# Masked graph attention: every second chunk of visits 6 to 21 transposed by VectorE, and wider weight buffers in visits 1 to 7

## The reference

```
h   = relu(layernorm(x))                                # row by row
e   = leaky_relu(h @ a[:256] + (h @ a[256:]).T, 0.01)   # 8192 x 8192
att = softmax(where(adj > 0, e, -9e15), axis=1)
out = x + att @ h
```

## Time and profile before

| | |
|---|---|
| median of 3 runs | 1552.14 us (1547.85 to 1553.05) |
| the profiled execution | 1552.08 us, of it span 1550.3 us |
| granted TensorE clock | 0.999 |
| PE busy | 1522.7 us, 98% |
| DVE busy | 1489.6 us, 96% |
| ACT busy | 1162.5 us, 75% |
| POOL busy | 457.4 us, 30% |
| DMA | 331.05 MB, mean 214 GB/s |

### The profile page before, as it was taken

The page is one execution under the profiler, slowest core; times in us unless marked ns, Lnnn a source line. Parts: engine busy times, 40 slices in busy tenths (PEclk is TensorE's granted clock), DMA queues, the critical chain, the costliest instruction groups (busy, mean ns, idle before and its releaser), DMA issues.

```text
span 1550.3 us, 38852 instructions
## 1 busy us (share of the span) xinstructions
PE 1522.7 (98%) x12678; PEld 1511.9 (98%) x12678; DVE 1489.6 (96%) x2172; ACT 1162.5 (75%) x1180; POOL 457.4 (30%) x547
## 2 busy tenths in 40 slices
PE   5999999999999999999999999999999999999999
PEld 5999999999999999999999999999999999999998
DVE  7999999999999999999999999999999999999998
ACT  7787877778777777677776876777777777677774
POOL 6363334335452340120420320320320320420420
PEclk9999999999999999999999999999999999999999
DMA  6666677787778799999999999999999999999994
GB/s 211 222 200 230 206 223 227 230 248 221 245 220 254 220 225 233 221 201 206 218 207 207 224 204 207 226 197 210 230 195 205 228 195 207 217 195 209 219 199 98
DMA packets 436493, 331.05 MB, mean 214 GB/s; under 512 B 16704, under 2 KB 378176, under 8 KB 436416
## 3 DMA queue, kind: packets, MB, share of 16 engines
q1 hardware_dynamic: 411360, 288.94, 83.6%
q10 hardware_dynamic: 25056, 41.13, 8.7%
HBM read 308.90 MB, written 21.10 MB: 213 GB/s over the span
## 4 chain that ended last, share of the span: by engine, by line
PE 82%; DMA 5%; DVE 3%; ACT 3%; issue 2%; SPq 1%; ACTq 0%; DVEq 0%
PE acc L950 27%; PE acc L953 26%; PE acc L952 26%; DMA adj_in<-in_adj_dram 5%; PE T L917 2%; ACT mask L542 2%; DVE w_lo L797 1%; DVE halves L786 1%; SPq L268 1%; ACT w_hi L552 0%; DVE T L767 0%; DVE w_lo L801 0%; ACT w_hi L555 0%; DVE adj_in L901 0%; DVE adj_in L896 0%
## 5 line engine op out<-in xcount | busy, mean ns | idle before, releaser
L950 PE MATMUL acc<-h_hi,w_hi 128*128 128x258 f32 (+1 forms) x4096 | 1167.3, 285 | 9.2 <-DVE w_lo L801 3.4
L953 PE MATMUL acc<-h_hi,w_lo 128*128 128x258 f32 (+1 forms) x4096 | 1153.3, 282 | 0.0
L952 PE MATMUL acc<-h_lo,w_hi 128*128 128x256 f32 (+1 forms) x4096 | 1149.7, 281 | 0.0
L950 PEld LDWEIGHTS acc<-h_hi,w_hi 128*128 128x128 f32 x4096 | 771.8, 188 | 17.8 <-issue 8.0
L952 PEld LDWEIGHTS acc<-h_lo,w_hi 128*128 128x128 f32 x4096 | 778.4, 190 | 0.1
L953 PEld LDWEIGHTS acc<-h_hi,w_lo 128*128 128x128 f32 x4096 | 775.3, 189 | 0.0
L786 DVE SCALAR_TENSOR_TENSOR halves<-r_rep,g_all,T 128x512 f32<-128x512 f32 (+1 forms) x1024 | 712.7, 736 | 10.8 <-PE T L917 1.5
L542 ACT ACTIVATE mask<-adj_in,mhalf 128x2048 fp8e5<-128x2048 int32 x256 | 510.3, 1993 | 58.8 <-DMA adj_in<-in_adj_dram 58.5
L552 ACT ACTIVATE w_hi<-halves 128x1024 fp32r<-128x1024 f32 x336 | 353.6, 1057 | 185.0 <-DVE halves L786 172.3
L797 DVE SCALAR_TENSOR_TENSOR w_lo<-halves,w_hi 128x1024 fp32r<-128x1024 f32 x336 | 418.2, 1245 | 9.9 <-PE acc L953 4.9
L555 ACT ACTIVATE w_hi<-halves 128x1024 fp32r<-128x1024 f32 x176 | 185.3, 1057 | 97.5 <-DVE halves L786 92.6
(11 more groups left out here) (70 smaller groups left out, 343.8 us busy)
## 6 DMA issues: line engine op xcount, KB each, us to landing
adj_in<-in_adj_dram SPq DMA_DIRECT2D x672, 256.0 KB, 5.0
adj_in<-in_adj_dram SPq DMA_DIRECT2D x88, 1024.0 KB, 6.3
part_sums<-stage ACTq DMA_DIRECT2D x24, 516.0 KB, 5.6
xo<-part_sums ACTq DMA_DIRECT2D x24, 516.0 KB, 4.4
r_rep<-r_rows SPq DMA_DIRECT2D x39, 256.0 KB, 4.8
xb<-in_x_dram ACTq DMA_DIRECT2D x15, 512.0 KB, 5.9
out_dram<-xb ACTq DMA_DIRECT2D x15, 512.0 KB, 4.7
xb<-in_x_dram SPq DMA_DIRECT2D x14, 512.0 KB, 5.8
```

The source lines that it names most:

```text
L950: nc.tensor.matmul(acc[:, t, 0:WC], w_hi[:, k % HL, cols], rhs_hi, start=start and u == 0, stop=False)
L952: nc.tensor.matmul(acc[:, t, 0:D], w_hi[:, k % HL, cols], rhs_lo, start=False, stop=False)
L953: last = nc.tensor.matmul(acc[:, t, 0:WC], w_lo[:, k % LL, cols], rhs_hi, start=False, stop=stop and u == 1)
```

## The change

In visits 6 to 21 (iterations 12 to 43) the odd chunk of each iteration is loaded in the order for VectorE and transposed by VectorE, in slot k = 1 between the subtraction (with side work) and the weights. TensorE keeps the even chunks. The forms have names now: PLAIN (TensorE both), ALT (TensorE even, VectorE odd), LATE (VectorE both); the counts that the semaphores are compared with are worked out from the form. In visits 1 to 7 (`wide`) the pairs' weights go to four pairs of halves instead of two buffers; the two halves more lie where `xo` is, so `halves` and `xo` are now one tensor `work`, and the scratch output of the row sums goes to a spare half of the PSUM bank `hs_ps` and into a weight buffer. The half with the older reader is written first (u = 1, then u = 0).

```diff
+    PLAIN, ALT, LATE = (0, 0), (0, 4), (4, 4)
+    N_ALT = 2 * 6
     N_MID = 2 * 22
+    def count_turned_by_tensor(n, kc, form):
+        return n * CI + kc + 1 if form == PLAIN else n + N_ALT + 1
+    def count_turned_by_vector(n, kc, form):
+        return n - N_ALT + 1 if form == ALT else N_MID - N_ALT + (n - N_MID) * CI + kc + 1
...
+        work = sb("work", [P, 8 * BLK + G * WC], f32)
+        halves = work[:, 0:10 * BLK].rearrange("p (n j) -> p n j", j=BLK)
+        xo = work[:, 8 * BLK:].rearrange("p (t w) -> p t w", w=WC)
+        wide_w = [halves[:, 2:4, :], halves[:, 4:6, :], halves[:, 2:9:6, :], halves[:, 4:10:5, :]]
...
             def quarter(v, q, prev, make=None, phase=None, made=None, nxt=None, head=False, turn=False,
-                        dt=MID, dt_next=MID, deep=False):
+                        dt=ALT, dt_next=ALT, deep=False, wide=False, pwide=False):
...
-                for q in range(4 if dt else 0):
-                    sp.dma_start(adj_in[32 * q:32 * q + 32, kc, G - dt:G, :],
-                                 adj_turned[b, :, 4 * (G - dt):4 * G, ds(c * BLK + q * P, P)]).then_inc(s_turn[kc], 16)
+                    sp.dma_start(adj_in[32 * q:32 * q + 32, kc, :, :],
+                                 adj_turned[b, :, :, ds(c * BLK + q * P, P)]).then_inc(s_turn[kc], 16)
...
-                    load_adj(V.b, c + kc, n, kc, not (V.head and first), V.dt)
+                    load_adj(V.b, c + kc, n, kc, not (V.head and first), V.dt[kc])
...
             def transpose_mask(V, n, kc):
-                g = n * CI + kc
-                t = G - V.dt
-                if V.dt < G:
-                    dve.wait_ge(s_T, g + 1)
-                else:
-                    dve.wait_ge(s_mask, g + 1)
+                dve.wait_ge(s_mask, n * CI + kc + 1)
                 dve.sem_inc(s_vgate, 1)
-                nc.vector.transpose(T[:, kc, t * P:], mask_words[:, kc, t:G, :]).then_inc(s_TV, 1)
...
+                nc.vector.transpose(T[:, kc, :], mask_words[:, kc, :, :]).then_inc(s_TV, 1)
+            def weights(V, c, n, g, k, wait, enter=False, scored=None):
...
-                if wait and (not V.deep or enter):
+                if wait and not V.wide and (not V.deep or enter):
                     dve.wait_ge(s_lo, g - 1)
...
-                for u in range(2):
+                for u in (1, 0) if V.wide else (0, 1):
                     e = 2 * (k % 2) + u
+                    if V.wide and u == 1:
+                        dve.wait_ge(s_lo, g - 1 if enter else g - 3)
+                    if V.wide and u == 0:
+                        dve.wait_ge(s_lo, g - 1)
+                        if scored is not None:
+                            dve.wait_ge(s_dot, scored)
...
-                enter = first and isinstance(V.v, int) and V.v == 22
+                enter = first and isinstance(V.v, int) and V.v in (1, 22)
...
-                        if V.dt and k % 2 == 0:
+                        if V.dt == LATE and k % 2 == 0:
                             transpose_mask(V, n, kc)
...
+                        if V.dt == ALT and k == 1:
+                            transpose_mask(V, n, 1)
+                        weights(V, c + kc, n, g, k, True, enter,
+                                2 * G * V.make + 2 * k + 4 if scored else None)
...
-                        transpose_mask(n + 1, kc, True, V.dt_next if last else V.dt)
+                        transpose_mask(n + 1, kc, True, (V.dt_next if last else V.dt)[kc])
```

More of the change, by code:

```diff
@@ L4 @@
 from collections import namedtuple
-Visit = namedtuple("Visit", "v n0 b c0 its prev pb f pa make phase made nxt head tail dt dt_next deep rest")
+Visit = namedtuple("Visit", "v n0 b c0 its prev pb f pa make phase made nxt head tail dt dt_next deep rest wide pwide")
 def masked_graph_attention(nc, x, adj, a, out):
@@ L217, in finals, with two @@
                             pa=2 * SH + m, make=None, phase=None, made=None, nxt=None if tail else m + 1,
[L218 to L225, removed]
+                            head=False, tail=tail, dt=LATE, dt_next=LATE, deep=True, rest=None, wide=False, pwide=False))
+            def two(j, q1, q2, prev1, prev2, nxt=None, dt=ALT, wide=(False, False, False)):
+                quarter(5 + 2 * j, q1, prev1, make=SH + j, phase="early", made=SH - 1 + j, nxt=nxt, dt=dt,
+                        wide=wide[1], pwide=wide[0])
+                quarter(6 + 2 * j, q2, prev2, make=SH + j, phase="late", turn=q2 != q1, wide=wide[2], pwide=wide[1])
+            quarter(0, 0, None, head=True, dt=PLAIN, dt_next=PLAIN)
+            quarter(1, 0, "first", make=Q, phase="whole", dt=PLAIN, dt_next=PLAIN, wide=True)
             with eng.Fori(2, 5) as v:
-                quarter(v, 0, "first", make=v + 3, phase="whole", made=v + 2, dt=0, dt_next=0)
-            two(0, 0, 0, "first", "first", dt=0)
-            two(1, 0, 1, "first", "first", nxt=0)
+                quarter(v, 0, "first", make=v + 3, phase="whole", made=v + 2, dt=PLAIN, dt_next=PLAIN, wide=True, pwide=True)
+            two(0, 0, 0, "first", "first", dt=PLAIN, wide=(True, True, True))
+            two(1, 0, 1, "first", "first", nxt=0, wide=(True, True, False))
             with eng.Fori(2, 5) as j:
@@ L529, in early_round_h, with convert @@
                                          scale=q4[:, parity, e:e + 1]).then_inc(s_hh if e == G - 1 else s_h0, 1)
-            def convert(n, kc, wait, dt):
-                if dt < G:
+            def convert(n, kc, wait, form):
+                if form[kc]:
+                    act.wait_ge(s_turn[kc], 64 * (n - FIRST_TURNED[kc] + 1))
+                else:
                     act.wait_ge(s_adj[kc], 16 * (n + 1))
[L535 to L538, removed]
+                was = form
+                if isinstance(n, int) and n == N_ALT and form == ALT:
+                    was = PLAIN
+                if isinstance(n, int) and n == N_MID:
+                    was = ALT
+                if wait and was[kc]:
+                    act.wait_ge(s_TV, count_turned_by_vector(n - 1, kc, was))
                 elif wait:
-                    act.wait_ge(s_T, n * CI + kc - 1)
+                    act.wait_ge(s_T, count_turned_by_tensor(n - 1, kc, was))
                 act.sem_inc(s_gate, 1)
@@ L544, in convert, with round_w @@
                                      ACT.Sign, bias=mhalf[:, 0:1], scale=1.0, saturate=False).then_inc(s_mask, 1)
-            def round_w(g, k, wait, deep=False):
+            def round_w(g, k, wait, slots=None):
                 act.wait_ge(s_w, g + 1)
@@ L753, in scores @@
                         dve.wait_ge(s_dot, 2 * G * c + 2 * e + j + 1)
+                        if free is not None and j == 1:
+                            dve.wait_ge(s_lo, free)
                         nc.vector.scalar_tensor_tensor(out[j], h[:, e, :], 1.0, a_ps[:, j * D:(j + 1) * D],
@@ L789, in weights, with subtract @@
                 last.then_inc(s_w, 1)
-            def subtract(g, k, wait, deep=False):
+            def subtract(g, k, wait, slots=None):
                 dve.wait_ge(s_hi, g + 1)
@@ L833, in _, with side_work, row_sums @@
             dve.wait_ge(s_r0, 1)
-            def side_work(V, k):
+            def side_work(V, k, g):
+                def row_sums(e):
+                    if V.wide:
+                        if isinstance(V.v, int) and V.v == 1 and e == 0:
+                            dve.wait_ge(s_hsum, Q)
+                        scores(V.make, 0, [e], [hs_ps[:, D:2 * D], wide_w[e][:, 0, 0:D]], g - 1)
+                    else:
+                        scores(V.make, 0, [e])
                 if V.phase == "whole":
@@ L842, in side_work @@
                     if k >= 4:
[L843 removed]
+                        row_sums(k - 4)
                 if V.phase == "early" and 1 <= k <= 4:
@@ L862, in steps @@
                         dve.wait_ge(s_ex, m + 1)
-                        weights(V, m, n * CI + kc, g, k, not (first and k < 2))
+                        weights(V, m, n, g, k, not (first and k < 2))
                         if m + 1 < Q:
```

62 lines of the change are left out of this document (31 added, 31 removed).

## The result

The changed kernel takes 1556.03 us in the median of 8 runs (1553.68 to 1559.41), the kernel before 1552.24 (1547.85 to 1555.48, 8 runs). The ratio is 1.0025 with a 95% interval of 1.0014 to 1.0036: 3.8 us slower. That is within the 0.3% that I had called no change, but a ratio of 1 lies outside the interval. The time has gone up where the forecast of 1549.2 had it go down, and out of the range of 1545 to 1555. The profiled execution took 1558.1 us, 2 us more than the median; its span of 1556.3 is 6.0 us longer than that of before.

A forecast was written before the change was run, and what follows sets the result against it. TensorE bounds visits 10 to 19 with VectorE close behind, and VectorE was to take over; VectorE bounds visits 1 to 4. Terms -1.1 - 3.8 + 1.7 + 0.3 = -2.9 take 1552.08 to 1549.2 us, range 1545 to 1555.

The forecast's parts named there:

- All that TensorE gives back is eaten: Visits 10 to 19: VectorE had 10.6 us to spare and gets 10.5 more; 247.7 us, +1.7.
- its own sign: The prediction's stated test for the whole kernel: it is wrong if the time leaves 1545 to 1555 us.
- visit 22 on: nothing is changed: Visits 22 on: no change counted, though waits for loads can fall otherwise, by +-2 us.
- The mask wait: Start of each late visit: VectorE's transpose waits for ScalarE's conversion of the odd chunk, 0.35 us once in two visits.
- the 0.07: Part of the transpose's wait for ScalarE's conversion: a semaphore's 0.07 us, an estimate, on top of 0.28.
- the ledger: The prediction's account of VectorE's time by slots: plain 2.65 us, row sums 3.13; a transpose adds 0.43 or 0.62.
- the 8.8 us: Visits 10 to 19: stretch of VectorE's subtractions beside GpSimd's tensor operations, 80 times 0.11 us.
- the longer of the two engines: Method for each stretch: its time is the longer of VectorE's and TensorE's; visits 5 to 9: 119.2 and 119.0, -3.8 us.
- The 0.19 us for each plain slot: Visits 2 to 4: wider buffers save VectorE's wait for its own subtraction, two plain slots per first iteration; -1.1 us.
- TensorE did not stay the bound: Rival, TensorE stays the bound: stretch halves, visits 10 to 19 take 241.5 us, 1541.6 in all; chance 0.28.
- The turned odd load: Rival, visits 6 to 21: odd chunks land late, ScalarE's conversion waits; one of three late gives 1559.9 us; chance 0.21.
- The rule of the Trainium skill: Rival: waiting for the engine's own last instruction costs nothing extra, so the 0.19 us is never saved; 1555.2 us, chance 0.04.

The follow-up runs named there:

- e2: The changed kernel with w_hi, w_lo, r_rep and ident laid ahead of work, at multiples of 512 bytes again; 1553.89 us, ratio 1.0007 to the kernel before.
- e5: e2 with GpSimd's sum of h rows and part-sum addition cut to one column each (sums wrong); 1544.26 us, ratio 0.9931 to the kernel before.
- e6: The kernel before with GpSimd's sum of h rows and part-sum addition cut to one column each (sums wrong); 1549.32 us, ratio 0.9985.
- e3: The wider weight buffers alone, in e2's layout, TensorE transposing every chunk up to visit 21; 1550.10 us, ratio 0.9988 to the kernel before.
- e1: The kernel before with only halves and xo merged, so w_hi, w_lo and r_rep start 4128 bytes later; 1554.31 us, ratio 1.0021.
- e4: Odd chunks by VectorE alone, with the layout and two weight buffers of the kernel before; 1554.49 us, ratio 1.0021 to the kernel before.
- e8: e2 with odd chunks by VectorE in visits 6 to 8 alone, TensorE for both in 9 to 21; 1546.22 us, ratio 0.9952 to the kernel before.

## Why the prediction was wrong

**What bounds the kernel** was read rightly: TensorE before, VectorE behind it with some 10 us to spare in visits 10 to 19, and the stretch where they meet GpSimd. "All that TensorE gives back is eaten" is what happened in visits 10 to 19. But the prediction is wrong by its own sign, the range of 1545 to 1555. The profiled execution is 8.9 us above 1549.2: +3.9 in visits 22 to 39, +2.3 in 5 to 9, +2.1 in 10 to 19, +0.5 in 20 and 21, +1.3 in the first visit and, to the other side, -1.2 in 1 to 4, which was luck. The step that failed most is "visit 22 on: nothing is changed", a term of 0; without it e2 is within its interval of no change. The others follow one by one.

**Visits 10 to 19: 249.8 us for 247.7.** The transposes cost nearly what was said: 0.40 and 0.60 us instead of 0.43 and 0.62, 10.0 in all and not 10.5. The mask wait comes where it was put, five times, at 0.44 us instead of 0.35. This is the conversion in visit 16:

```profile
422.79 1.99 ACT L561 ACTIVATE mask<-adj_in,mhalf 128x2048 fp8e5<-128x2048 int32 x1
```

It ends at 424.78, 0.28 us after the transpose could have started (423.37 + 1.13), as forecast; but the transpose starts 0.16 us behind that end, at 424.94, where I had estimated 0.07 for the semaphore. No run shows the 0.07. GpSimd's addition of the part sums is awaited once (0.6), which I had not listed. And the stretch, taken as unchanged, grew: 1342 ns less 1330, 80 times, is 1.0 us. -0.5 + 0.45 + 0.6 + 1.0 is 1.6 of the 2.1 that were missing; the rest is in steps some hundredths longer than the ledger's. The step that failed is the one that kept the 8.8 us fixed, though I had written that a VectorE without idle time meets GpSimd more often. e5 prices most of it (a mean of 1242 ns is left, and 1220 is undisturbed), e6 shows that it was free before.

**Visits 5 to 9: 121.5 us for 119.2.** Here the method failed, not a size: "the longer of the two engines" over five visits. The two are coupled, by two `w_lo` buffers and by ScalarE's roundings between them, so VectorE can't use the time of an easy iteration in a hard one. In visit 6 it first waits (0.64 us before 185.20, for a rounding), and then its second iteration takes 13.1 us (185.20 to 198.34) without any wait, where TensorE needs 11.9. The subtraction waited 2.4 + 0.4 us in this stretch and TensorE was idle for 1.2. (GpSimd has a share here too: e5 takes 120.3 us for these visits and e2 121.5, and 0.8 of the difference is visit 9, where GpSimd adds part sums again.) The sums may be compared only over stretches that the buffers between the engines can even out. Rows of the changed kernel in visit 6:

```profile
185.20 1.23 DVE L823 SCALAR_TENSOR_TENSOR w_lo<-work,w_hi 128x1024 fp32r<-128x1024 f32 x1 [0.64 <-ACT w_hi L571]
188.34 1.22 DVE L823 SCALAR_TENSOR_TENSOR w_lo<-work,w_hi 128x1024 fp32r<-128x1024 f32 x1
190.16 0.73 DVE L785 STREAM_TRANSPOSE T<-mask 128x512 f32<-128x512 f32 x1
...
198.34 1.22 DVE L823 SCALAR_TENSOR_TENSOR w_lo<-work,w_hi 128x1024 fp32r<-128x1024 f32 x1
```

**Visits 1 to 4: -2.3 us for -1.1.** The 0.19 us for each plain slot is right (e3). Left out was that a subtraction at another moment misses GpSimd, the same mechanism as above to the other side (0.30 us, e3 and e6), and a second wait in the first slot that I had not looked at.

**Visits 22 to 39: "nothing is changed" was wrong.** The diff changes the place of `w_hi`, `w_lo`, `r_rep` and `ident` by merging two tensors, and TensorE's pace with it: by 0.11 us in a visit of two iterations that hangs on it (22.90 for 22.79), and by 0.3 in one of eight (the fastest takes 91.63 us in the changed kernel, 91.65 in e1 and 91.35 before). For visits 24 to 39 that makes some 3.3 us as an estimate, eight times 0.11 and eight times 0.3, if all hung on it. e1 measures 1 to 5 us for the places alone (2.1 between the medians), and e2 is 2.1 us below the changed kernel. This term, which I had not looked for, is by the medians 2.1 of the 3.8 us: e2 is at 1.0007, and its interval includes no change. Of the 3.9 us of the profiled execution 2.7 lie in visits 24 to 39 and 1.3 in visits 22 and 23, which grow in every kernel that turns the odd chunks up to visit 21.

**The first visit's +1.3 us** is of this one execution. TensorE's granted clock over the window 20 to 27 us was 0.56 there and 0.76 before, that is longer at the lower level, with the same work ahead of it. Visit 0 took 36.4 us here and 35.2 to 35.4 in each of the eight experiments.

**The rivals.** TensorE did not stay the bound. Its rival was also priced amiss: 241.5 us for visits 10 to 19 are VectorE's steps with half the stretch, 4 us over TensorE's 237.2, so by its own sum VectorE would still have been the bound. e5, with most of GpSimd's sums gone, took 241.6. The turned odd load did not come late: in visits 6 to 21 ScalarE waited 0.6 us in all for adj, at a DMA share of 0.90 in visits 10 to 19 (the prediction had said 0.95, where the mean of its two rows is 0.91). The rule of the Trainium skill had been priced at 1555.2, near the time that was measured, and is contradicted by e3's steps all the same: a time can agree with a wrong mechanism.

In sum, by the ratios: the wider buffers -1.9 us (e3), the transposes +3.3 (e4), the buffers' places +3.3 (e1) make +4.7, each within some 2 us; by the medians -2.2, +2.2 and +2.1 make +2.1. 3.8 was measured, between the two.

**What stays open.** Which of the moved buffers costs TensorE the 0.5%, and whether it is the remainder of 32 bytes that 4128 leaves: e1 and e2 move several at once. The buffers `one` and `xb` are out, since e2 leaves them at their new places. The 1.3 us of visits 22 and 23 go with the transposes up to visit 21, but that loads make them rests on the trace's word, not on a run that takes the loads away. And the 2 us of e8 beyond what its visits up to 21 gain are unexplained.

## What to carry to other kernels

When the diff merges or resizes a buffer, those allocated behind it can move; put the two layouts beside each other before writing "unchanged". Work shifted from the bound to an engine with x us to spare gains only as long as it adds less than x, and the spare time must be counted per iteration, not per stretch, when two buffers couple the engines. And a contention that costs nothing today is a cost that the change switches on: price it with the cover gone. The best version here, e8, takes the transposes only where GpSimd is idle enough.

## What the runs showed of the hardware

- The same 192 matmuls with buffers 4128 bytes further on took 22.90 us instead of 22.79, to the hundredth in visits 28, 30, 32, 34 and 38 of two kernels (the changed one and e1); with the weight buffers back at multiples of 512 bytes it was 22.79. In visits 5 to 20 of e1, where TensorE also transposes, the difference was only 0.03 us a visit.
- A wait for the engine's own last instruction cost VectorE 0.19 us between two instructions of 1.2 and 0.7 us (slots of 2.65 us for 2.45), and nothing with an instruction of 0.4 us or more between them: with one statistic the slot took 2.77 us, and the statistic itself 0.34 from start to start.
- VectorE's subtraction of two operands in SBUF took 1.22 us alone and up to 1.84 beside GpSimd's tensor operations (visits 10 to 19 of the kernel before; 1.78 in the changed one); the transposes and weights, which read PSUM or write to it, kept 0.70 to 0.73 and 0.70 to 0.75 us in the same visits.
- VectorE's transpose started 0.16 us after the end of the ScalarE conversion that it waited for (424.94 behind 424.78 in the changed kernel).
